# Attention with V as the held operand instead of the exponentials

## What is computed

```python
q = conv2d(inp, wq); k = conv2d(inp, wk, 1, 1); v = conv2d(inp, wv, 1, 1)   # 256 = 8 heads x 32
q = q * cos + rotate_every_two(q) * sin                                      # k likewise
dots = jnp.einsum('bhid,bhjd->bhij', q, k) * SCALE                           # 1024 x 1024 per head
attn = jax.nn.softmax(dots, axis=-1)
attn = jnp.einsum('bhij,hg->bgij', attn, mix)
out = jnp.einsum('bhij,bhjd->bhid', attn, v)
o = conv2d(out, wo) + bo[None, :, None, None]
a, g = jnp.split(o, 2, axis=1)
return a * jax.nn.sigmoid(g)
```

## Time and profile before

| What | Value |
|---|---|
| median of 3 runs | 3080.15 us |
| the profiled execution's own time | 3081.93 us |
| its span, first to last instruction | 3080.2 us |
| TensorE matmul busy | 2951.5 us, 96% |
| VectorE busy | 2193.4 us, 71% |
| ScalarE busy | 1446.3 us, 47% |
| GpSimd busy | 1331.2 us, 43% |
| granted TensorE clock, mean | 0.986 |

### The profile page before, as it was taken

One profiled execution on the slowest core, in us unless ns is written; L12 is line 12 of the kernel. 1 busy time (PEld: TensorE's weight loads), 2 busy tenths in 40 slices (PEclk: granted clock), 3 DMA queues, 4 the chain that ended last, 5 costly groups with the idle time before them and its releaser, 6 DMA issues.

```text
span 3080.2 us, 54552 instructions
## 1 busy us (share of the span) xinstructions
PE 2951.5 (96%) x20354; PEld 2717.5 (88%) x20354; DVE 2193.4 (71%) x3332; ACT 1446.3 (47%) x1862; POOL 1331.2 (43%) x996
## 2 busy tenths in 40 slices
PE   8999999999999999999999999999999999948996
PEld 6999889998999899988999899979998899837776
DVE  4677768775877587776877687758776787655663
ACT  2455335542555255534554355525552455436671
POOL 3244424542454334542454245433454246227783
PEclk9999999999999999999999999999999999969998
DMA  3364010101110101101010111010110111127665
GB/s 116 132 230 153 5 41 22 44 10 35 30 30 25 36 22 23 40 16 32 22 46 9 35 32 30 23 36 22 25 39 19 28 32 52 50 92 264 232 223 206
DMA packets 71429, 196.94 MB, mean 64 GB/s; under 512 B 16136, under 2 KB 16722, under 8 KB 71158
## 3 DMA queue, kind: packets, MB, share of 16 engines
q1 hardware_dynamic: 62070, 176.40, 18.7%
q0 software_dynamic: 9088, 16.94, 1.7%
HBM read 40.43 MB, written 63.34 MB: 34 GB/s over the span
## 4 chain that ended last, share of the span: by engine, by line
PE 89%; issue 4%; ACT 3%; DMA 2%; DVE 2%; POOL 1%; SPq 0%; POOLq 0%; ACTq 0%; DVEq 0%
PE PV L629 49%; PE ST L629 25%; PE MX L629 13%; DMA wt<-wall 1%; ACT h L1003 1%; ACT xr L1003 1%; DMA wall<-yrows 0%; ACT E L1003 0%; PE PV L759 0%; PE PV L717 0%; DVE El L1304 0%; POOL yrows L597 0%; PE MX L932 0%; PE PV L948 0%; DVE mcol L1299 0%
## 5 line engine op out<-in xcount | busy, mean ns | idle before, releaser
L515 POOL TENSOR_TENSOR acc<-acc,tmp 128x256 f32<-128x256 f32 x512 | 802.3, 1567 | 1372.2 <-DVE tmp L1314 1372.2
L629 PE MATMUL PV<-vh,El 128*128 128x258 f32 x4096 | 1185.2, 289 | 11.9 <-DVE vl L1294 7.9
L629 PE MATMUL PV<-vh,Eh 128*128 128x258 f32 x4096 | 1154.5, 282 | 0.0
L629 PE MATMUL PV<-vl,Eh 128*128 128x256 f32 x4096 | 1149.9, 281 | 0.0
L1003 ACT ACTIVATE Eh<-ST 128x1024 fp32r<-128x1024 f32 x512 | 524.9, 1025 | 765.4 <-PE ST L629 765.4
L1299 DVE TENSOR_REDUCE mcol<-MX 128x1 fp32r<-128x1024 f32 x512 | 625.8, 1222 | 348.7 <-PE MX L629 346.5
L629 PEld LDWEIGHTS PV<-vh,El 128*128 128x128 f32 x4096 | 772.5, 189 | 43.3 <-DVE El L1304 8.8
L629 PEld LDWEIGHTS PV<-vl,Eh 128*128 128x128 f32 x4096 | 778.0, 190 | 24.5 <-issue 3.8
L629 PEld LDWEIGHTS PV<-vh,Eh 128*128 128x128 f32 x4096 | 772.6, 189 | 0.0
L1304 DVE TENSOR_TENSOR El<-E,Eh 128x1024 fp32r<-128x1024 f32 x512 | 632.2, 1235 | 9.9 <-ACT E L1003 9.8
L1003 ACT ACTIVATE E<-ST 128x1024 f32<-128x1024 f32 x512 | 521.6, 1019 | 0.0
(11 more groups left out here) (219 smaller groups left out, 3154.1 us busy)
## 6 DMA issues: line engine op xcount, KB each, us to landing
rows<-xr SPq DMA_DIRECT2D x68, 520.0 KB, 5.7
kst<-src SPq DMA_DIRECT2D x192, 128.0 KB
qst<-src SPq DMA_DIRECT2D x192, 128.0 KB
wt<-wall SPq DMA_DIRECT2D x39, 514.0 KB
wt<-wall SPq DMA_DIRECT2D x39, 512.5 KB
xrow<-rows SPq DMA_DIRECT2D x39, 260.0 KB
wall<-yrows SPq DMA_DIRECT2D x32, 256.0 KB, 4.6
xr<-in_x_dram SPq DMA_DIRECT2D x9, 512.0 KB, 3.6
```

Of the source, the lines that this page charges most:

```text
L515: nc.gpsimd.tensor_tensor(acc[:, ic, :], acc[:, ic, :], tmp[:, p, :], ALU.add).then_inc(s_acc, 1)
L629: return nc.tensor.matmul(o, w, m, start=start, stop=stop)
```

## The change

A unit is now one head and 512 queries: 16 units an image (`UNITS`, `NB`), in 8 key chunks `kc` of 128. TensorE holds a 128 x 128 block of V (vh or vl), and 512 queries of exponentials stream past it. Results are transposed (output channel by query), in the two halves PV[0] and PV[1] of the tensor PVT, and no transposes of acc follow. There is no column of ones: the sum of the exponentials must be known beforehand. ScalarE therefore exponentiates the scores of `max_scores` too, in place in PSUM and with a summed output (`sums`, 4 per unit, 128 x 1024 each). VectorE computes minus the maximum and minus the logarithm of the sum with 14 small instructions (`shifts`) and splits it into a high and a low part. TensorE turns those into two rows (`max_row`), which ScalarE copies into rows 97 and 98 of the stacked queries. So the exponentials come out normalised.

Further: ScalarE computes each exponential once, into float32, in four buffers of 512 queries; GpSimd rounds it to float32r (`cast`); VectorE subtracts as before. ScalarE takes the results out of PSUM with mix as the scale (`evict`), into acc for the two units of head 0 and into tmp otherwise, and GpSimd adds them. The six banks of scores become MA, MB (two each) and ST (one each). Routing steps and scatters stand in the first half of an image's units. The attention scale is folded into wq. The first and the last image are written out beside the loop; the last does not prepare a next image.

```diff
-            def add(n, k, p):
-                ic = k % QC * 2 + p
-                wait(pool, s_nrm, 2 * n + p + 3)
-                wait(pool, s_acc, 2 * n + p + 2)
-                nc.gpsimd.tensor_tensor(acc[:, ic, :], acc[:, ic, :], tmp[:, p, :], ALU.add).then_inc(s_acc, 1)
+            def cast(b, u, kc):
...
+                nc.gpsimd.tensor_copy(Eh[:, kc, :], E32[:, kc % 4, :]).then_inc(s_eh, 1)
...
+            def unit(b, u, prev):
+                for kc in range(KC):
...
+                    if u < UNITS - 1:
+                        cast(b, u + 1, kc)
+                    if kc == 1 and u >= 3:
+                        for c in range(2):
+                            add(b, u - 1, c)
...
+                    if prev is not None and 4 <= u < 8 and kc % 2 == 1:
+                        scatter(prev, 4 * u - 16 + kc // 2)
```

TensorE's list (`values`, `scores` and the unit):

```diff
+            def scores(b, u, kc):
+                n, (par, cols) = b * UNITS + u, heads_of(u)
+                if kc == 0:
+                    pe.wait_ge(s_mrow, n + 1)
+                wait(pe, s_ex, KC * n + kc - 1)
+                mm(ST[kc % 2][:, :], kst[par][:, kc * P:(kc + 1) * P], qst[par][:, cols], True, True).then_inc(s_st, 1)
+            def max_row(b, u, free):
+                n = b * UNITS + u
+                wait(pe, s_ch, NCH * n + NCH)
+                wait(pe, s_l, free)
...
+            def values(b, u, kc):
+                pe.wait_ge(s_lo, KC * n + kc + 1)
+                for c in range(2):
...
+                    last = split3(PV[c], vh[:, kc, cols], vl[:, kc, cols], Eh[:, kc, :], El[:, kc, :], kc == 0, kc == KC - 1)
...
+            def unit(b, u, prev, more):
+                for kc in range(KC):
+                    values(b, u, kc)
+                    if u < UNITS - 1:
+                        scores(b, u + 1, kc)
+                    if kc == 1:
+                        if u < UNITS - 2:
+                            max_scores(b, u + 2, 2, MA, 4 * n + 9)
...
+                    if kc == 3 and u < UNITS - 2:
+                        max_scores(b, u + 2, 3, MB, 4 * n + 10)
+                    if kc == 5:
+                        if u < UNITS - 3:
+                            max_scores(b, u + 3, 0, MA, 4 * n + 11)
...
+                    if kc == KC - 1:
+                        if u < UNITS - 2:
+                            max_row(b, u + 2, 4 * n + 13 if u < UNITS - 3 else 4 * n + 11)
+                        if u < UNITS - 3:
+                            max_scores(b, u + 3, 1, MB, 4 * n + 12)
```

ScalarE's and VectorE's:

```diff
+            def sums(b, u, i, M):
+                act.wait_ge(s_red, 4 * n + i + 1)
+                copy(M[:, :], M[:, :], ACT.Exp, bias=nmax[:, par, i:i + 1], accum_out=rsum[:, par, i:i + 1]).then_inc(s_l, 1)
+            def exps(b, u, kc):
+                wait(act, s_lo, KC * n + kc - 3)
+                act.wait_ge(s_st, KC * n + kc + 1)
+                copy(E32[:, kc % 4, :], ST[kc % 2][:, :], ACT.Exp).then_inc(s_ex, 1)
...
+            def unit(b, u, prev, more):
+                for kc in range(KC):
+                    if kc == KC - 1:
+                        for c in range(2):
+                            evict(b, u, c)
+                        if u < UNITS - 2:
+                            row_copy(b, u + 2)
+                    if u < UNITS - 1:
+                        exps(b, u + 1, kc)
...
+                    if kc == 4 and u < UNITS - 2:
+                        sums(b, u + 2, 3, MB)
+                    if kc == 6 and u < UNITS - 3:
+                        sums(b, u + 3, 0, MA)
...
+            def shifts(b, u, part):
+                if part == 0:
+                    dve.wait_ge(s_l, 4 * n + 4)
+                    ts(m.bitcast(i32), bits, 0x007fffff, 0x3f800000, ALU.bitwise_and, ALU.bitwise_or).then_inc(s_ch, 1)
...
+                if part == 1:
+                    dve.wait_ge(s_ch, base + 6)
+                    stt(m, m, -ROOT, q, ALU.add, ALU.mult).then_inc(s_ch, 1)
+                    dve.wait_ge(s_ch, base + 7)
+                    tt(y, m, m, ALU.mult).then_inc(s_ch, 1)
...
+                if part == 2:
+                    wait(dve, s_mt, n - 1)
+                    dve.wait_ge(s_ch, base + 12)
+                    nc.vector.tensor_copy(mc[:, par, :, 0], z).then_inc(s_ch, 1)
+                    dve.wait_ge(s_ch, base + 13)
+                    tt(mc[:, par, :, 1], z, f(mc[:, par, :, 0]), ALU.subtract).then_inc(s_ch, 1)
...
+            def unit(b, u, prev, more):
+                for kc in range(KC):
...
+                    if u < UNITS - 2 and kc == 6:
+                        shifts(b, u + 2, 1)
+                    routed(0)
+                    if kc == 0:
+                        exp_lo(b, u, KC - 1)
+                    elif u < UNITS - 1:
+                        exp_lo(b, u + 1, kc - 1)
+                    if u < UNITS - 2 and kc == 5:
+                        shifts(b, u + 2, 0)
+                    if u < UNITS - 2 and kc == 6:
+                        shifts(b, u + 2, 2)
+                    if u < UNITS - 2 and kc in (1, 3):
+                        take_max(b, u + 2, 2 + kc // 2, MA if kc == 1 else MB)
+                    if u < UNITS - 3 and kc in (5, 7):
+                        take_max(b, u + 3, kc // 2 - 2, MA if kc == 5 else MB)
+                    routed(1)
```

917 lines of the change are left out of this document (468 added, 449 removed).

## The result

The changed kernel takes 3449.34 us (median of 4 runs, 3443.15 to 3449.73) against 3082.27 us (median of 4 runs, the three of the table above and one more, 3077.63 to 3094.12): ratio 1.118, 95% interval 1.1145 to 1.1214. The forecast was 3306 us in a range up to 3430: the sign was right, and 143 us were missing.

What follows compares the result with a forecast made beforehand. TensorE, busy for 96% of the span, was taken to bound the kernel. Own work, row chain, port, scatters, routing and prologue gave 3080 - 63 + 67 + 101 + 42 + 21 + 58 = 3306 us, range 3030 to 3430.

Steps and rivals of the forecast that it cites:

- TensorE's own work: Wider matmuls for V product and scores, no transposes of acc, no input gap: -63 us together, 3018 without new waits.
- The 14 us for the gap: TensorE's 1.96 us gap before an image's first convolution goes 7 times, as the next input is ready earlier: -14.
- The wait for the row: TensorE waits at max_row in 112 units: 0.6 us for the chain (+67) and 0.9 for port blocking (+101).
- The port's part: GpSimd's casts of chunks 5 and 6 each hold a small VectorE instruction 0.45 us: 0.9 a unit, +101.
- The scatters: GpSimd's indirect DMAs in units 4 to 7 make the cast of chunk 4 late: 1.5 us in 28 units, +42.
- The routing: Routing steps at every chunk of units 0 to 2, two inside the chain: 1.0 us in 21 units, +21.
- The starts: New TensorE waits in the prologue of each image: 7.3 us in each of 8, +58.
- The parts a, b and c: Waits in each start: 2.3 us after the last matmul, 2.7 for shared bank MA, 2.3 for unit 1's shifts.
- The clock: TensorE's new waits were taken as too short to cost clock; no time was added.
- GpSimd bound: Rival: casts cost 1.3 us like two-input operations, so GpSimd becomes the bound: about 3570 us, chance 0.12.
- Chain without port: Rival: the new chain to max_row costs its wait but VectorE and GpSimd do not block each other: 3161 us, chance 0.25.
- Faster: Rival: the other engines run far enough ahead that max_row finds its rows ready, no new wait: 3018 us, chance 0.13.

Runs made afterwards that it cites:

- experiments 7, 9 and 12: e_prol, e_start, and a second order of the images' starts alone (first score block behind conv 7, second gate later) against the changed kernel: 3359 us, ratio 1.0901.
- Experiment 4: Surplus 512-column matmuls, results unread, put in TensorE's waits ahead of the row matmuls of the changed kernel: 3393 us, ratio 1.1007.
- the best order: Changed kernel with scatters, score blocks, small steps and additions reordered in the units, plus the second order of the images' starts: 3188 us, ratio 1.0347.
- e_row: Changed kernel with the next unit's row matmuls and row copy issued one chunk later: 3535 us, ratio 1.1464.
- e_early: Changed kernel with score block 0 and its sum one chunk earlier and the small shift steps in one piece: 3501 us, ratio 1.1358.
- e_prol: Changed kernel with the previous image's second output projection behind conv 6 and unit 1's row through MB: 3471 us, ratio 1.127.
- e_start: Changed kernel with the images' starts reordered: gate behind rotations 4 and 5, score blocks from conv 6 on, second projection in conv 7: 3445 us, ratio 1.1175.
- edits 2, 6 and 7: Scatters moved to chunks 5 to 7 of units 4 to 9 (alone 3400 us), e_early and e_prol; together, with additions apart, on the changed kernel: 3303 us.

## Why the prediction was wrong, point by point

- **TensorE's own work, -63.** More was gained than this. The unit stands: one with next to no wait took 15.3 us, as forecast. But over the V matmuls of the attention stages at full clock and with no gap before them, the median distance of starts is 0.119 us before, as taken, and 0.229 after, for 0.233 (a price from the expert layer); the means are 0.122 and 0.231. By these the product with V gives some 60 to 75 us (an estimate), not 30. The 14 us for the gap of the earlier trace rows were wrong. It was read as the wait for the input; behind the same place, where nothing is waited for, it is still there and longer:

```profile
1911.96 0.80 PE L654 MATMUL ST<-xh,wql 128*128 128x512 f32 x1 [2.85 <-issue]
```

  The gap belongs to the jump back to the start of the loop. The changed kernel has it at five starts (2.17 to 2.85 us), those that follow a jump back, and at neither of the two that lie at the loop's ends; the kernel before has it at six of seven (1.46 to 1.96), all but the one that enters the loop. So it was 9.8 us in all before, not 14, and is 13.0 now.
- **The wait for the row, 1.5 us a unit (+67 and +101).** Right in sum, 1.5 to 1.64. The mechanism is right too: the casts hold small steps, one each. The port's part was mis-sized, 0.52 us a unit in the mean for 0.9; a later start of the chain (3.0 us for 2.3) made up for it, in part by the additions, which had no term here. That the sum came out is luck as far as its parts go.
- **The scatters, 1.5 us in each of 28 units.** Mis-sized: 3.2 us, and 1.3 more in unit 8, some 55 us more in all. Only the issues' own time was counted, not that the late chain brings the lower clock into the units (8 or 9 slow matmuls each in units 5 to 7).
- **The routing, 1.0 us in 21 units.** Less: 0.4 to 0.7 us in units 1 and 2 against the first image, some 8 us in all, the lower bound of the forecast.
- **A term left out.** The next image's normalisation stands in units 12 to 14. In the last image, which prepares none, these take 45 us, elsewhere 52: some 50 us in seven images, of which TensorE's own added matmuls are under 2 us each time. In the kernel before all waits of TensorE over 0.4 us in the eight attention stages were 18 us together.
- **Why the attention stages agree.** By the gaps over 0.4 us TensorE's waits there grew from 18 to 224 us, 206 where 231 were forecast; the lower clock adds the estimated 68; TensorE's own work fell by the rest, some 117, where 35 were forecast (60 to 75 by the product with V, 5 by the scores, and some 30 that now stand in the starts, by the estimates here). The sum is +157 measured and +196 forecast, so these stages were 39 us better than forecast, by errors that cancel.
- **The starts, 7.3 us each.** The step that failed. With the 1.8 us of transposes and the 2.0 of the gap that the sum also gives back, it allows a start 3.5 us more than before (the 81 of the forecast leave these savings out); 26.7 came. Seven times the 23 us that lack are 162, and 15 of the 22 ahead of the first V matmul come on top; less the 39 of the attention stages, that is 138 of the 143. The parts a, b and c were priced one by one where each stands. What the changed trace shows is waits of 17 us (2.4 before): in the start shown 2.85 at the jump, 4.1 for the gate, 3.5 for score blocks, 6.5 for the row of unit 1. Part a, 2.3 us for the input of the first projection, is there in the two starts without a jump (2.3 us); in the others the jump covers it. To the waits come 7 us of extra matmul time at the lower clock and some 4.6 us of added work, which is what is left of the 26.7. Most of that work was overlooked and is only moved: units 0 and 1 are twice as large as before and half of unit 2 is there as well, so 20 matmuls of `max_scores` stand ahead of the first V matmul for 8, and the 8 of `scores` have twice the columns. At 0.233 and 0.119 us that is 3.7 us a start (an estimate), which the attention stages no longer have. The waits belong to one chain, through gate, rotation 4, stacks and nine blocks in one bank, which experiments 7, 9 and 12 show: the start can be shortened by 12 us with the same work.
- **The clock.** Priced at nothing, by one window with a gap of 1.96 us in it; some 120 us of extra matmul time over the kernel before. Experiment 4 shows that it follows the waits.
- **The rivals.** "GpSimd bound" is out (0.625 us a cast). "Chain without port" is out too: every one of the 112 chains has a stretched step. "Faster" is out, for no plain unit is without the wait.

What is left in the best order's start, 14 us over that of before: 7 us of waits (9.4 for 2.4), 4 us of the lower clock, and the 3.7 us of moved work. Open: whether an order without these waits exists; none was tried. Open too is how much of the 50 us of the normalisation order can take away.

## What to carry to other kernels

When the lists of several engines are written anew, walk the whole start of a stage as one chain over all engines, in the order of each queue. Single edits often moved a wait or cost time here (e_row +85, e_early +52, e_prol +22, e_start nothing). In the starts only the head of the chain, moved with its followers, gained (90 us). In the attention stages edits 2, 6 and 7, alone -49, +52 and +22, made -146 together with the additions apart. Look behind a wait for the one that it covers before removing it. Count what moves from one stage into another. And price a stall of some microseconds on TensorE at more than its length.

## What the runs showed of the hardware

- TensorE's lower clock set in with waits in the middle of a busy kernel, in 61 stretches between the first and the last V matmul, nearly all of 3.4 or 6.8 us; 1004 surplus matmuls in the waits made the kernel 56 us faster.
- A cast on GpSimd (128x512, 0.625 us) holds a dependent 128x4 instruction of VectorE until it ends: 182 of them took 0.41 to 0.60 us instead of 0.17, and each ended 0.01 to 0.03 us behind a cast. With the cast of chunk 6 shortened, one stretched step was gone in nearly each chain.
- VectorE's reciprocal of 128x512 takes 3.35 us, 5 times a multiplication of that size (0.69), and everything behind it in VectorE's list waits that long.
- An accumulating activation on ScalarE brings a second instruction, 0.2 us (`ACTIVATION_READ_ACCUMULATOR`), that its reader waits for.
- The jump back in the loop over the images leaves TensorE idle for 2.17 to 2.85 us (1.46 to 1.96 in the kernel before), between the first and the second matmul of the changed loop's body; the starts outside the loop have no such gap.
